# The gated delta rule of a two-layer model, from chunks of 128 tokens to chunks of 64 with both batches in the partitions

## The reference

```python
qkvz = hidden_states @ W_qkvz            # 256 -> per key head: q, k (128 each), v, z (256 each)
y = silu(conv1d(concat(q, k, v), conv_w))    # causal, 4 taps, a weight per channel
beta = sigmoid(b); g = -exp(A_log) * softplus(a + dt_bias)
q = l2norm(q) * DK ** -0.5; k = l2norm(k)    # each shared by two value heads
def step(S, inp):                        # for every batch and value head, token by token
    S = S * exp(gt)
    kv = einsum('hk,hkv->hv', kt, S)
    delta = (vt - kv) * bt
    S = S + kt[:, :, None] * delta[:, None, :]
    o = einsum('hk,hkv->hv', qt, S)
gated = core * silu(z)
gated = gated * rsqrt(mean(gated * gated) + EPS) * norm_w
out = gated @ W_out
```

## Time and profile before

| | |
|---|---|
| median of 3 runs | 3025.31 us (3024.3 to 3028.1) |
| span of the profiled execution | 3029.8 us |
| TensorE busy | 2869.1 us (95%) |
| VectorE | 2236.9 us (74%) |
| ScalarE | 1953.1 us (64%) |
| GpSimd | 1556.2 us (51%) |
| DMA queue, share of 16 engines | 21.9% |
| full slots of `delta_rule` | from about 400 to 2600 us |

### The profile page before, as it was taken

One profiled execution on the slowest core, in us unless ns is written; L12 is line 12 of the kernel. 1 busy time (PEld: TensorE's weight loads), 2 busy tenths in 40 slices (PEclk: granted clock), 3 DMA queues, 4 the chain that ended last, 5 costly groups with the idle time before them and its releaser, 6 DMA issues. The chain is left out here.

```text
span 3029.8 us, 70798 instructions
## 1 busy us (share of the span) xinstructions
PE 2869.1 (95%) x22765; PEld 2139.7 (71%) x22765; DVE 2236.9 (74%) x4805; ACT 1953.1 (64%) x6436; POOL 1556.2 (51%) x3618
## 2 busy tenths in 40 slices
PE   5999499999999999999999999999999999879998
PEld 4556267777777777777777777777777777755555
DVE  3443478888888888888888888788888888636776
ACT  3322467777777777777777777777777777532332
POOL 2000466666666666666666666666666666510000
PEclk9999699999999999999999999999999999979999
DMA  3000222223222322222222223222222232110000
GB/s 87 1 1 0 59 62 55 59 52 62 52 59 52 65 63 62 57 55 60 54 62 49 64 55 70 56 60 52 61 53 60 52 63 64 34 43 1 7 8 14
DMA packets 482423, 147.47 MB, mean 49 GB/s; under 512 B 352592, under 2 KB 481216, under 8 KB 482048
## 3 DMA queue, kind: packets, MB, share of 16 engines
q1 hardware_dynamic: 482048, 142.81, 21.9%
HBM read 97.40 MB, written 45.35 MB: 47 GB/s over the span
## 5 line engine op out<-in xcount | busy, mean ns | idle before, releaser
L944 ACT ACTIVATE raw<-bank 128x512 f32<-128x512 f32 x256 | 152.9, 597 | 376.7 <-PE bank L704 335.1
L499 POOL TENSOR_TENSOR Tb<-Tb,btmp 64x14 f32<-64x14 f32 (+6 forms) x896 | 315.6, 352 | 70.9 <-POOL btmp L495 1.1
L495 POOL TENSOR_TENSOR btmp<-Bk,Tb 64x14 f32<-64x14 f32 (+6 forms) x896 | 269.8, 301 | 65.3
L1215 DVE SCALAR_TENSOR_TENSOR conv<-raw,ckq,conv 128x512 f32<-128x512 f32 x384 | 261.6, 749 | 22.1 <-ACT conv L945 20.2
L1215 DVE SCALAR_TENSOR_TENSOR conv<-raw,cv,conv 128x512 f32<-128x512 f32 x384 | 264.2, 753 | 9.8 <-ACT conv L945 7.8
L704 PE MATMUL bank<-xnT,wkq 128*128 128x512 f32 x512 | 253.8, 620 | 13.6 <-POOL mkX L393 7.2
L484 POOL TENSOR_TENSOR Tb<-Bk,lower 64x256 f32<-64x256 f32 x64 | 58.6, 916 | 402.9 <-issue 397.8
L704 PE MATMUL bank<-xnT,wv 128*128 128x512 f32 x512 | 250.5, 612 | 9.4 <-issue 9.4
L772 PE MATMUL bank<-wout_h,gT 128*128 128x256 f32 x1024 | 245.6, 383 | 0.1
L1184 DVE SCALAR_TENSOR_TENSOR S<-S,gs,bank 128x128 f32<-128x128 f32 x512 | 143.8, 343 | 134.2 <-PE bank L743 134.2
L720 PE MATMUL bank<-wz_h,xnT 128*128 128x256 f32 x1024 | 242.4, 380 | 0.0
(11 more groups left out here) (354 smaller groups left out, 7569.6 us busy)
## 6 DMA issues: line engine op xcount, KB each, us to landing
rowb<-decay_rows SPq DMA_DIRECT2D x128, 256.0 KB, 5.1
blk_n<-N SPq DMA_DIRECT2D x128, 256.0 KB, 3.1
Tp<-blk_t SPq DMA_DIRECT2D x128, 128.0 KB, 2.9
Wp<-blk_w SPq DMA_DIRECT2D x128, 128.0 KB, 3.0
wkq<-in_L_attn_W_qkvz_dram SPq DMA_DIRECT2D x32, 128.0 KB, 2.3
wv<-in_L_attn_W_qkvz_dram SPq DMA_DIRECT2D x16, 256.0 KB, 2.7
Bk<-blk_n SPq DMA_DIRECT2D x64, 64.0 KB, 2.7
blk_t<-Tb SPq DMA_DIRECT2D x64, 64.0 KB, 2.5
```

The costliest lines, as they stand in the source:

```text
L495: pool.tensor_tensor(tmp, Bk[:, j, j + 1:].unsqueeze(2).broadcast_to([64, 15 - j, j]), Tb[:, j, 0:j].unsqueeze(1).broadcast_to([64, 15 - j ...
L499: pool.tensor_tensor(Tb[:, j + 1:, 0:j], Tb[:, j + 1:, 0:j], tmp, ALU.subtract).then_inc(row_rdy, 1)
L944: act.activation(raw[h][:, j, :, 3:], bB[1 - j], ACT.Copy)
L1215: dve.scalar_tensor_tensor(out=conv[h][:, j], in0=raw[h][:, j, :, k:k + 256], scalar=cw[:, j, k:k + 1], in1=conv[h][:, j], op0=ALU.mult, o ...
```

## The change

A step now has its 128 tokens as two chunks of 64 (index h or s), and the two batches lie side by side in the partitions: 64 partitions for each. The step and its four units stay; a unit is now (chunk, value head), with both batches in it. 128 steps as before.

- N, attention and the decay products are 64x64 for each chunk and batch; the tiles `ET`, `ETm`, `N`, `attn`, `rowb` halve to 128x256. The inverse ends at 64x64: `x64`, `w64`, `xev64`, `wev64` and the four extra products of `w3` go.
- The recurrence runs twice a slot: `keys(h)`, `queries(h)`, `rhs(h)`, `solve(h)`, `uscale(h)`, `increment(h)`, `update(h)` for h = 0 and 1. `update` is four multiply-adds each time, `rhs` two. Products for the two batches stand in pairs on the two halves of the array: by output partitions (128 rows, 64 columns: `keys`, `queries`, `causal`), by both (64x64: `solve`, `attend`, the inverse), by rows (64x128: `increment`).
- `strict` is one product of 128x256 instead of four multiply-adds; its factor comes from a new GpSimd function `scaled` (`ETn`).
- The lags S_L, S_D, S_E become 6, 7, 8 (136 slots), the rings of N, attn, kd, vb 8 deep; `vb` lies in `xn`. `zz` has two buffers; `ztanh` and the tanh of `silu` move to the end of ScalarE's slot, of the step that is one slot younger.
- `raw` and `conv` hold four quarters of 64 tokens; `evac` has a third copy of 128x18 for the quarters' halos.
- Each engine's list has a new order. Dumps of N and loads of `rowb` are two DMAs of half the partitions, the decay rows are written by four DMAs.
- `front` makes `xnT` at once in the order that is needed; the copy `xnS` and GpSimd's 16 copies go. The gate sums are four products instead of three.

The diff, cut to its core:

```diff
-    S_P, S_S, S_F, S_L, S_D, S_E = 0, 1, 2, 5, 6, 7
-    RING = 4
+    S_P, S_S, S_F, S_L, S_D, S_E = 0, 1, 2, 6, 7, 8
+    RING = 8
...
                 def dump(s):
-                    sp.dma_start(units(nd, U * (t.c % 2), U), N[t.c % RING][:]).then_inc(n_out, 16)
+                    for b in range(B):
+                        sp.dma_start(matrices(nd, U * (t.c % 2), U, b), N[t.c % RING][half[b]]).then_inc(n_out, 16)
...
+                def scaled(s):
+
+                    t = s.back(S_F)
+                    if not t.live:
+                        return
+                    pool.wait_ge(exp_rdy, t.done())
+                    pool.wait_ge(der_rdy, t.done())
+                    wait(pool, N_rdy, t.done(1))
+                    pool.tensor_tensor(ETn[:], ET[:], ty[t.c][:, CC, :].unsqueeze(2).broadcast_to([P, U, H]),
+                                       ALU.mult).then_inc(ETn_rdy, 1)
...
                 def out_scale(s):
 
-                    t = s.back(S_D)
+                    t = s.back(S_E)
...
                 def body(s):
                     step_gates(s)
+                    out_scale(s)
                     derive(s)
+                    scaled(s)
                     causal(s)
                     halo(s)
                     base_rest(s)
                     base_first(s)
-                    out_scale(s)
                     norm_scale(s)
                 pipeline(pool, body)
...
+                def keys(s, h):
 
                     t = s.back(S_D)
                     if not t.live:
                         return
+                    wait(pe, S_rdy, t.part(h, 1))
+                    for b in range(B):
+                        i = pe.matmul(bank[6][half[b], 0:256], kq_of(t)[:, 0, quarter(t, h), b, :],
+                                      S[:, 2 * b:2 * b + 2, :].rearrange("p v n -> p (v n)"), start=True, stop=True)
+                    i.then_inc(ks_mm, 1)
...
+                def increment(s, h):
...
+                    pe.wait_ge(Us_rdy, t.part(h))
+                    pe.wait_ge(oq_rdy, t.part(h))
+                    for v in range(2):
+                        for b in range(B):
+                            i = pe.matmul(pKU[b][:, v], kd[t.c % RING][half[b], 2 * h + v, :], Us[half[b], 2 * h + v, :],
+                                          start=True, stop=True)
+                    i.then_inc(up_mm, 1)
...
                 def body(s):
                     front_tp(s)
-                    state_in(s)
-                    x64(s)
+                    keys(s, 0)
+                    queries(s, 0)
+                    causal(s)
                     x16(s)
-                    causal(s)
+                    solve(s, 0)
+                    project(s, 0)
+                    increment(s, 0)
                     w1(s)
-                    w64(s)
-                    project(s, 0)
-                    solve(s)
+                    values(s)
+                    project(s, 1)
+                    keys(s, 1)
+                    queries(s, 1)
                     w2(s)
-                    values(s)
-                    apply(s)
-                    project(s, 1)
-                    w3(s)
+                    solve(s, 1)
                     gated_tp(s)
                     zproj(s)
                     low_rank(s)
+                    increment(s, 1)
+                    attend(s)
+                    w3(s)
                     project_out(s)
                     norm_tp(s)
                 pipeline(pe, body)
...
                 def squares(s):
 
-                    t = s.back(S_D)
+                    t = s.back(S_E)
...
-                    act.activation(raw[h][:, j, :, 3:], bB[1 - j], ACT.Copy)
-                    act.activation(conv[h][:, j], bB[1 - j], ACT.Copy,
+                    new = bank[1 - j][:].rearrange("p (c b n) -> p c b n", c=4, b=B)
+                    act.activation(raw[h][:, j, :, :, 3:], new, ACT.Copy)
+                    act.activation(raw[h][:, j, 1:4, :, 0:3], new[:, 0:3, :, H - 3:], ACT.Copy)
+                    act.activation(conv[h][:, j].rearrange("p c b n -> p (c b n)"), bank[1 - j][:], ACT.Copy,
                                    scale=(cv if h else ckq)[:, j, 3:4]).then_inc(braw_rdy if j else araw_rdy, 1)
...
                 def body(s):
-                    ztanh(s)
+                    squares(s)
                     norms(s)
-                    silu(s)
-                    xev64(s)
-                    from_state(s)
+                    from_state(s, 0)
                     normed(s)
-                    wev64(s)
                     evac(s, 0)
                     vscale(s)
                     kdec(s)
                     evac(s, 1)
+                    from_state(s, 1)
                     gtev(s)
-                    squares(s)
                     clamp(s)
                     expo(s)
+                    ztanh(s)
+                    silu(s)
                     low_rank_ev(s)
                     norm_ev(s)
                 pipeline(act, body)
...
                 def body(s):
                     gate(s)
+                    rhs(s, 0)
+                    silu(s)
+                    xev16(s)
+                    uscale(s, 0)
                     accumulate(s)
-                    rhs(s)
-                    xev16(s)
-                    silu(s)
+                    update(s, 0)
                     add_w1(s)
+                    tap(s, 0, (2, 1))
                     strict(s)
-                    uscale(s)
+                    rhs(s, 1)
+                    attention(s)
+                    uscale(s, 1)
                     add_w2(s)
-                    update(s)
+                    tap(s, 0, (0,))
+                    tap(s, 1, (2, 1, 0))
+                    update(s, 1)
+                    add_w3(s)
                     output(s)
-                    attention(s)
-                    add_w3(s)
-                    taps(s)
                     norm_apply(s)
                     norm_stats(s)
                 pipeline(dve, body)
```

More of the change, by code:

```diff
@@ L386, in _ @@
                 for u in range(U):
-                    last = pool.tensor_copy(le4[:, u, :], m["le"][:])
+                    last = pool.tensor_copy(le4[half[0], u, :], m["le"][half[0], half[0]])
+                last.then_inc(le4_rdy, 1)
+                pool.wait_ge(le4_rdy, 1)
+                for u in range(U):
+                    last = pool.tensor_copy(le4[half[1], u, :], m["le"][half[1], half[1]])
                 last.then_inc(setup, 1)
@@ L571, in x16 @@
                     wait(pe, t_in, loaded)
+                    c = last_chunk(s, S_E + 5)
+                    if c is not None:
+                        pe.wait_ge(qk_out, c + 1)
                     for u in range(U):
-                        for h in (slice(0, 64), slice(64, P)):
-                            i = pe.matmul(bH[5][h, u], Nt[h, u, h], T[h, u, :], start=True, stop=True)
+                        for h in half:
+                            i = pe.matmul(bH[5][h, u], Nt[h, u, :], T[h, u, :], start=True, stop=True)
                     i.then_inc(x16_mm, 1)
@@ L586, in w1 @@
                     wait(pe, xs_rdy, done)
-                    wait(pe, xs64_rdy, before)
+                    wait(pe, w3_rdy, before)
                     for u in range(U):
-                        for h in (slice(0, 64), slice(64, P)):
+                        for h in half:
                             i = pe.matmul(bH[4][h, u], Xs[h, u, :], W[h, u, :], start=True, stop=True)
@@ L654, in front_tp @@
                     wait(pe, kd_rdy, t.done(1))
+                    wait(pe, gT_rdy, t.done(S_E + 1 - S_F))
                     for j in range(2):
-                        for b in range(B):
-                            i = pe.transpose(bU[2][:, 2 * j + b], chunk(y, t, j, b), m["ident"][:])
+                        for h in range(2):
+                            i = pe.transpose(bU[2][:, 2 * j + h], y[:, j, quarter(t, h)].rearrange("p b n -> p (b n)"), m["ident"][:])
                     i.then_inc(kq_tp, 1)
@@ L665, in causal @@
                     y = kq_of(t)
-                    wait(pe, N_rdy, t.done(1))
                     wait(pe, attn_rdy, t.done(1))
-                    for b in range(B):
-                        i = pe.matmul(bB[3][:, b], chunk(y, t, 0, b), y[:, :, b, (t.c % 2) * P:(t.c % 2 + 1) * P],
-                                      start=True, stop=True)
+                    wait(pe, o_rdy, t.done(S_D + 1 - S_F))
+                    for h in range(2):
+                        for b in range(B):
+                            i = pe.matmul(bank[3][half[b], P * h:P * h + P], y[:, 0, quarter(t, h), b, :], y[:, :, quarter(t, h), b, :],
+                                          start=True, stop=True)
                     i.then_inc(gram_mm, 1)
@@ L699, in project @@
                     else:
-                        wait(pe, zz_rdy, min(t.done(6), STEPS) if t.i is None else t.done(6))
```

(14 more changed lines are left out.)

443 lines of the change are left out of this document (215 added, 228 removed).

## The result

The changed kernel takes 3647.58 us (median; 3639.41 to 3648.85), the kernel before, measured beside it, 3026.7 us: ratio 1.204, interval 1.202 to 1.206. The direction and the mechanism were forecast; the size was not. The forecast was 3475 us, its upper end 3600.

A forecast was written before the change was run, and what follows sets the result against it. A once-per-slot loop across engines, not TensorE, was to bound the changed kernel: 10.0 + 10.2 = 20.2 us, plus 1.4 for the clock, 21.6. 120 x (21.6 - 17.96) = 437, and 12, on 3029.8: 3479, so 3475; range 3235 to 3600.

The forecast's parts named there:

- The loop: Wait cycle through ScalarE, GpSimd, TensorE and VectorE, closing once per slot: 20.2 us without the clock, against TensorE's 18.0.
- The first half, 10.0: From `gat_rdy` to the start of `project(1)` (T), through `squares`, GpSimd's operations and halo, `evac(0)`, `vscale`: 10.0 us.
- The second half, 6.3: VectorE's work in order from `uscale(1)` to `gat` done, including four convolution taps: 6.3 us.
- the clock, "I take 1.4": TensorE's clock halves after a 3.6 us gap ahead of `project(1)` in most slots, adding 1.4 us: slot 21.6.
- TensorE's own work, 16.6: TensorE's steps in a new slot without idleness: 15.23 us plus 1.36 for eight tile changes, 16.6.
- that rival: Loop, and the column pairs on TensorE take turns instead of overlapping: slot 22.5, 3582 us; chance 0.10.
- The clock holds: Rival: the loop bounds the slot but TensorE's clock does not fall: slot 20.2, 3306 us; chance 0.22.
- Only the `vscale` wait: Rival: GpSimd keeps out of the way, only `project(1)`'s wait for `vscale` remains: slot 18.0, 3042 us; chance 0.09.
- Faster: Rival: TensorE stays the bound and `vb` is ready in time for `project(1)`: slot 16.6, 2874 us; chance 0.09.
- the second chain: Block inverse holding GpSimd up at every other slot's start: 0.8 us every second slot, kept for the range only.

The follow-up runs named there:

- experiment 1: Changed kernel with GpSimd's halo copy moved to the first place in its slot, nothing else moved: 3173 us, ratio 1.049 to the kernel before.
- experiment 2: Changed kernel with seven extra, unread products on TensorE between `values` and `project(1)`: 3404 us, ratio 1.126 to the kernel before.
- experiment 9: experiment 4 with the block inverse's rows on GpSimd and its SyncE transfers one slot later or more, `dump` ahead of them: 2969 us, ratio 0.981.
- 10: experiment 9 with SyncE issuing the weights first in the slot, then the inverse's second load, then the block's load: 2932 us, ratio 0.968.
- experiment 3: Changed kernel with halo first and `out_scale` behind `causal` on GpSimd, `normed` behind `kdec` on ScalarE: 3091 us, ratio 1.022 to the kernel before.
- experiment 4: experiment 3 plus `project(1)` behind `solve(1)`, `from_state(1)` ahead of `evac(1)`, `rhs(1)` directly behind `add_w1`: 3064 us, ratio 1.014 to the kernel before.
- 7: Kernel before the change with TensorE's `values` moved behind `apply`, directly ahead of `project(1)`: 3234 us, ratio 1.070.

## Why the prediction missed the size

**The loop: right.** Its links were named in order, and experiment 1 shows that the halo's place closed it. Its length without the clock was forecast at 20.2; with the 4.07 of experiment 2 for the way from T to `uscale(1)` it is 10.28 + 4.07 + 6.50 = 20.85.

**The first half, 10.0: 10.28.** In the slot shown, `squares` 1.39 for 1.36; from their end to `scaled` 5.01 for 4.6; `scaled` 0.57 and `causal` 0.67 for 0.65 each; the halo and handing over 0.28 for 0.19; `evac(0)` 1.13 for 1.3; `vscale` 1.29 for 1.19. GpSimd's small operations, 0.4 over, are the larger part. L512 takes 1.09 us while VectorE runs `silu` with both inputs in SBUF (1517.99 to 1519.21). The same operation in experiment 9, there L513 and without such a neighbour, takes 0.20:

```profile
1510.27 0.20 POOL L513 TENSOR_SCALAR ty<-ty 128x4 f32<-128x4 f32 x1 [0.16 <-POOL ty L510]
```

The Trainium skill, "GPSIMD Engine Reference", section "1. Specifications", says that GpSimd's way to SBUF is shared with VectorE and contended when VectorE's instruction has two SBUF inputs; the trace agrees, with 1.09 against 0.20 us. Between 600 and 3000 us of the changed kernel 104 of 521 such operations (L456, L461, L509, L512, L517) ran for more than 0.1 us beside the `silu`, the taps or the last product of `gat`, which have two inputs in SBUF, and took 0.91 to 1.18; the other 417 took 0.19 to 0.23. The row behind the 4.6 held such company too (L466 at 0.64), so this is part of the 0.4 and need not be all of it.

**The second half, 6.3: 6.50.** One slot earlier it is 6.34 (1510.07 to 1516.41), and the four taps take 2.90, the sum of the forecast's 0.67, 0.67, 0.78 and 0.78:

```profile
1510.07 0.43 DVE L1179 TENSOR_TENSOR Us<-bank,ty 128x256 f32<-128x256 f32 x1 [1.21 <-PE bank L762]
...
1510.74 2.98 DVE L1246 SCALAR_TENSOR_TENSOR conv<-raw,ckq,conv 128x512 f32<-128x512 f32 x4
1513.64 1.12 DVE L1215 SCALAR_TENSOR_TENSOR S<-S,gs,bank 128x128 f32<-128x128 f32 x4
```

In the slot shown above the four take 3.49 (1532.94 to 1536.43), and `uscale(1)` to `gat` done is 6.92. There GpSimd works on the block inverse beside them from 1533.13 on, where it is idle beside the other four, and its small operations are slow too (this one takes 0.22 in experiment 1, from 1492.60):

```profile
1535.88 0.71 POOL L538 TENSOR_TENSOR btmp<-Bk,Tb 64x26 f32<-64x26 f32 x1
```

So the contention runs both ways: between 600 and 3000 us all 315 taps beside an idle GpSimd took 0.74 or 0.75 us, those beside a busy one up to 1.42.

**The step that failed: the clock, "I take 1.4".** I bounded the loss by `project(1)` (1.6) and "as much again if the low clock lasts to `solve(1)`", and took less than the first of these because "some falls will come early in the gap and be over sooner". None was over when `project(1)` began: from T to `keys(1)` it is 2.3 to 3.7 us in every one of the 109 slots, where it is 1.9 in all of experiment 2. In 51 of them all of `project(1)` runs at half clock (3.7 us), and then the small products behind it do too, as from 1503.00 to 1509.00 above. From T to `uscale(1)` it is 6.20 us against 4.07 without the low clock (experiment 2): the term was 2.1, not 1.4, mis-sized by 0.7 us. Over 120 slots that is 88 of the 159 us by which the span exceeds the sum. The rest is the loop, 0.65 longer than summed (0.28 in the first half, 0.2 in the second, and 0.17 of handing over and tile changes between T and `uscale(1)`), another 78; together a little over the 159, since the slots of filling and draining are shorter. Either miss alone would have stayed below the upper end of 3600 (3475 + 88, 3475 + 78); both together did not.

The Trainium skill, "TensorE: Matmul & The Clock Gate", Part 1, has the clock halved after an idle stretch and restored by sustained work; the trace agrees at 3.65 us, where it stays at 0.50 from 1503 to 1509.

**TensorE's own work, 16.6: 17.0.** The column pairs run together: `keys(0)` takes 0.48 to 0.53 and `queries(0)` 0.43, where one behind the other would have been 0.86. So that rival is out. A small set with its tile change costs 0.51 to 0.65; the forecast had 0.45, or 0.62 with a change. The changed work is worth 1.0 us a slot, and experiments 9 and 10 show it.

**The rivals.** "The clock holds" fails by the granted 0.89. "Only the `vscale` wait" came true in experiment 3 (18.4, not 18.0), and in 82 of 110 full slots of experiment 1. "Faster" needed `vb` in time, which experiment 4 gave, and the inverse out of the way, which 9 gave.

**What the second chain costs.** Priced at nothing in the forecast, since the loop's idleness hides it. That was right for the changed kernel, where the fifth row of the inverse ends at most 1.1 us into its slot, and for experiment 3. It was wrong for experiments 1 and 4, where it ends 1.5 to 4.2 and 4.1 to 6.5 us into it and slots of over 20 us come with it.

## What to carry to other kernels

When a whole order is rewritten, follow each buffer's release round the slot across all engines until it meets itself: where the sum of that loop exceeds the work of the busiest engine, it is the slot, and the link to cut can be a 0.2 us copy at the wrong end of a queue. Then look for the next one in the idle times of the run without it: here five changes, one on top of the other (experiments 1, 3, 4, 9 and 10), turned 1.20 into 0.968. Price a recurring gap that lowers the clock with the full low-clock time of the product behind it (here 1.8 us more) and something for what follows: 2.1 was lost on average.

## What the hardware showed that I had not expected

- Gaps on TensorE of 1.3 to 1.4 us in every slot left the clock at 1.00 (experiments 3 and 7, 1000 to 1500 us), and all of 3.55 to 4.28 us in the changed kernel lowered it. Between 1.9 and 3.1 us it went both ways: full behind 2.10 us and behind the 3.09 below (experiment 1), half behind 2.43 (experiment 4), and behind 2.18 with one of 1.56 shortly ahead of it (experiment 9). The length of one gap does not decide it. The low clock then lasted for 3.3 us of work (from 1526.75) or some 6 (from 1503.08): gaps of 3.76 cost 2.1 more each.

```profile
1542.95 1.96 PE L732 MATMUL bank<-xnT,wkq 128*128 128x512 f32 x4 [3.09 <-ACT xn L975]
```

- GpSimd's 128x4 operations: 0.20 us alone, 0.91 to 1.18 in the changed kernel beside VectorE's instructions with two SBUF inputs; VectorE's taps, 0.75 alone, up to 1.42 beside GpSimd. In a chain of nine such steps, 5.0 us long, one slow step was 0.9 of them.
- Products of 128 rows by 64 outputs on the two halves of the array overlap: two of 256 columns take 0.43 to 0.53 us, where they would take 0.86 in turn.
